# Local attention: which of two engines copies which head's transposed probabilities

## What is computed

```
h = layernorm(x)
lin_out = linear_attention(h @ wq_lin + bq_lin, h @ wk_lin + bk_lin, h @ wv_lin + bv_lin)
win_out = window_attention(h @ wq_loc + bq_loc, h @ wk_loc + bk_loc, h @ wv_loc + bv_loc, rel_bias)
gate = sigmoid(relu(concat(lin_out, win_out, h) @ wg1 + bg1) @ wg2 + bg2)
y = (gate * lin_out + (1 - gate) * win_out) @ wo + bo + h_input

window_attention, 16 heads of 8, window 64:
  scores[w] = sum_d(q * k shifted by w - 32) / sqrt(8) + rel_bias      (w = 0..64, -inf outside)
  attn = softmax over w
  out  = sum_w attn[w] * (v shifted by w - 32)
```

## Time and profile before

| | us |
|---|---|
| median of 3 runs | 2643.94 (2643.81 to 2646.72) |
| the profiled execution, device time | 2649.69 |
| its span, first to last instruction | 2646.9 |
| TensorE busy in it | 2476.4 (94%) |
| VectorE busy | 1937.0 (73%) |
| ScalarE busy | 1616.3 (61%) |
| GpSimd busy | 1147.0 (43%) |

### The profile page before, as it was taken

The page is one execution under the profiler, slowest core; times in us unless marked ns, Lnnn a source line. Parts: engine busy times, 40 slices in busy tenths (PEclk is TensorE's granted clock), DMA queues, the critical chain, the costliest instruction groups (busy, mean ns, idle before and its releaser), DMA issues. The chain is left out here.

```text
span 2646.9 us, 37817 instructions
## 1 busy us (share of the span) xinstructions
PE 2476.4 (94%) x11190; PEld 1413.2 (53%) x11190; DVE 1937.0 (73%) x3923; ACT 1616.3 (61%) x3503; POOL 1147.0 (43%) x924
## 2 busy tenths in 40 slices
PE   7999989899999999999989999988879998899977
PEld 5767754455555555555434444466644445556655
DVE  7888867799999999999956445466634444587754
ACT  4565533688888888888833344477734443466644
POOL 1000012499999999999930002022200001354532
PEclk8999989899999999999999999999989998999999
DMA  2000024344444444444443211000011110000000
GB/s 109 1 1 1 0 88 97 116 162 162 162 166 161 161 161 160 160 161 160 160 147 75 102 75 64 1 1 1 1 49 64 64 64 28 1 1 0 1 1 17
DMA packets 34771, 205.70 MB, mean 78 GB/s; under 512 B 4016, under 2 KB 5168, under 8 KB 13360
## 3 DMA queue, kind: packets, MB, share of 16 engines
q1 hardware_dynamic: 34608, 203.83, 21.7%
HBM read 201.19 MB, written 2.62 MB: 77 GB/s over the span
## 5 line engine op out<-in xcount | busy, mean ns | idle before, releaser
L1512 POOL TENSOR_TENSOR mam_state_c<-mam_state,weights_r 128x1024 f32<-128x1024 f32 x256 | 599.8, 2362 | 11.0 <-DVE mam_state L1474 9.8
L1474 DVE TENSOR_TENSOR_SCAN mam_state<-banks,mam_dbu 128x1024 f32<-128x1024 f32 x256 | 577.0, 2274 | 2.2 <-ACT banks L1543 1.3
L1593 PE MATMUL banks<-mam_state_c,identity 128*128 128x512 f32 x1024 | 483.2, 604 | 13.5 <-POOL mam_state_c L1512 12.9
L1543 ACT ACTIVATE banks<-mam_dt,mam_a_neg 128x255 f32<-128x255 f32 x1024 | 425.0, 461 | 64.3 <-DVE mam_state L1474 63.8
L1593 PEld LDWEIGHTS banks<-mam_state_c,identity 128*128 128x128 f32 x1024 | 186.5, 190 | 226.2 <-issue 189.6
L1021 PE MATMUL banks<-route_xnt,weights_r 128*128 128x512 f32 x512 | 245.0, 602 | 1.9 <-PEq L732 1.1
L1457 DVE TENSOR_TENSOR mam_dbu<-banks,weights_r 128x1024 f32<-128x1024 f32 x192 | 227.5, 1198 | 0.0
L432 ACT ACTIVATE at_probs<-banks,at_nmax 128x256 f32<-128x256 f32 x256 | 117.7, 472 | 139.4 <-DVE at_nmax L373 139.4
L552 POOL TENSOR_SCALAR route_ln_rs<-route_ln_mv 128x4 f32<-128x4 f32 x16 | 5.1, 317 | 453.0 <-DVE route_ln_mv L630 453.0
L2695 POOL TENSOR_TENSOR at_attention<-at_relu 128x512 f32<-128x512 f32 x128 | 131.0, 1040 | 127.3 <-ACT at_relu L2740 85.7
L969 DVE TENSOR_TENSOR m2b_hidden<-m2b_gelu,m2b_comb_spread 128x512 f32<-128x512 f32 x120 | 80.7, 690 | 116.4 <-ACT m2b_gelu L999 113.8
(11 more groups left out here) (433 smaller groups left out, 5027.8 us busy)
## 6 DMA issues: line engine op xcount, KB each, us to landing
weights_r<-mam_bc_rows SPq DMA_DIRECT2D x128, 1024.0 KB, 4.7
m2a_comb_spread<-m2a_comb_rows SPq DMA_DIRECT2D x15, 1024.0 KB, 6.9
m2b_comb_spread<-m2b_comb_rows SPq DMA_DIRECT2D x15, 1024.0 KB, 7.8
m1a_comb_spread<-m1a_comb_rows SPq DMA_DIRECT2D x14, 512.0 KB, 7.6
m1b_comb_spread<-m1b_comb_rows SPq DMA_DIRECT2D x14, 512.0 KB, 7.3
weights_r<-in_mb SPq DMA_DIRECT2D x1, 4332.0 KB, 13.0
weights_r<-in_m SPq DMA_DIRECT2D x1, 4200.0 KB, 12.8
weights_r<-in_a SPq DMA_DIRECT2D x1, 2632.0 KB, 11.9
```

Source lines behind the costliest of these rows:

```text
L1474: dve.tensor_tensor_scan(flat2(h[:, i % 4, :, :, :]), decay(i), flat2(dbu[:, i % 4, :, :, :]), 0.0, ALU.mult, ALU.add).then_inc(h_ready, 1)
L1512: pool.tensor_tensor(hc[:, j % 4, :, :, :], h[:, j % 4, :, :, :], c_rows(j), ALU.mult).then_inc(hc_ready, 1)
L1543: i = act.activation(decay(j)[:, o + 1:o + S], dt[:, q, c, 1:S], ACT.Exp, scale=aneg[:, l, k:k + 1])
L1593: k = pe.matmul(y_bank(q)[:, :], K.ident[:, :], flat(hc[:, j % 4, n, :, :]), start=(j == 0 and n == 0), stop=(j == NP - 1 and n == 1))
```

## The change

`BY_DVE`, the heads that VectorE copies, becomes the odd heads. Before they were 1, 4, 6, 9, 12 and 14 of each sequence; now they are 1, 3, 5, 7, 9, 11, 13 and 15. `BY_ACT` is what is left, so ScalarE copies the even heads, 0 to 14, in place of 0, 2, 3, 5, 7, 8, 10, 11, 13 and 15. As head h is transposed into bank 4 + h % 2, VectorE now reads bank 5 alone and ScalarE bank 4 alone. The slots, the copies' shapes and the banks stay. `wait_copied` and the two waits ahead of the product with the values go by these tuples and follow.

```diff
         TAIL = 15
-        BY_DVE = tuple(h for h in range(H) if h % 8 in (1, 4, 6))
+        BY_DVE = tuple(h for h in range(H) if h % 2)
         BY_ACT = tuple(h for h in range(H) if h not in BY_DVE)
```

## The result

The changed kernel takes 2668.45 us, the median of its four runs (2666.98 to 2669.76), against 2643.94 for the kernel before. A few executions of either kernel run in a slower state (one of before took 2927.95 us), and all medians and ratios here are of the others. A second comparison on another occasion gave 2665.79 us and 1.0084 (1.0071 to 1.0097), or 22.2 us. The forecast was 2661.5 in a range from 2649 to 2674. Sign and range held; of 22 to 25 us it had found 17.8. The profiled execution of the second comparison took 2660.96 us, the shortest of its six, so the traces show less of the loss than the medians do.

A forecast was written before the change was run, and what follows sets the result against it. The prediction took TensorE as pacer, in fixed order, standing still where VectorE or ScalarE comes late. Its terms, 10.0 + 0.4 + 7.4 = 17.8 us on the median 2643.94, gave 2661.5 us, range 2649 to 2674.

The forecast's parts named there:

- Slots 13 to 0, +1.0: Head 11's copy delays head 14's reduction; with head 12's copy on ScalarE, masked keys and next scores come 1.0 us later.
- Slots 0 to 4, +1.05: Head 15's copy delays the key-value sum; slot 4's scores come 2.0 us later, 1.0 of it already there at slot 0.
- The term of 5 x 2.0: Slot 13 to slot 4 costs 2.0 us in each of five sequence changes that are no loop boundary.
- Slots 5 to 7, +0.95: Copies of heads 3 and 4 delay ScalarE's output rows, the gate's first product and slot 8's scores: 0.95 us per sequence.
- 8 to 10, +0.1: Head 6's copy precedes the layer norm's output on ScalarE, but the gate's activation loses head 7's: 0.1 us per sequence.
- The boundaries, 2 x 0.2: Slots 13 to 4 at two loop boundaries: 0.2 us each, as TensorE's own delay covers most of VectorE's; bounds -1.3, +2.0.
- The eighth sequence and the tail, 0 with bounds of 0.6: First sequence and tail change copies only where a swap costs what it gives: nothing, bounds -0.6 to +0.6 us.
- The rival that saw the level fall in every sequence: TensorE's new pauses lower its clock in every sequence, 9.5 us more over five sequences: 2671 us, chance 0.2.
- only the two loop boundaries fall so far: Argument against the clock falling in every sequence: until now TensorE's level falls at the two loop boundaries alone.
- Absorption: Only the delay behind head 15 holds, 1.5 us in five sequences; ScalarE's reordered copies cost nothing: 2652 us, chance 0.15.
- relieved where it was late: ScalarE makes masked keys 0.48 us earlier and boundaries lose their wait on head 14: -9.8 us, 2634 us, chance 0.08.
- something moved: Answers the rival that nothing moves, swaps cancelling or only busy times balancing: 2644 us, chance 0.07.

The follow-up runs named there:

- second profile of after: The changed kernel, unchanged, run and traced once more: 2665.79 us, ratio 1.0084 to the kernel before.
- the experiment with head 15 alone: The kernel before, with only head 15's copy moved from ScalarE to VectorE: 2647.99 us, ratio 1.0014.
- head 15 back: The changed kernel with head 15's copy returned to ScalarE: 2660.28 us, ratio 1.0057 to the kernel before.
- heads 11 and 12 back: The changed kernel with head 11's copy returned to ScalarE and head 12's to VectorE: 2661.01 us, ratio 1.0054 to the kernel before.
- the keys moved with head 13 for 14: The kernel before with all masked keys in slot 14, the layer norm's output in slot 3, head 13 copied by VectorE and 14 by ScalarE: 2645.97 us.
- eight copies elsewhere: The kernel before with VectorE copying heads 1, 4, 5, 6, 7, 9, 12 and 13: 2644.71 us, ratio 1.0005.
- the second profile of before: The kernel before, unchanged, run and traced once more: 2643.56 us, ratio 0.9996.
- the kernel with head 13 for 14: The kernel before with head 13's copy moved to VectorE and head 14's to ScalarE: 2646.79 us, ratio 1.0006.

## Why the prediction was right, and where its sum fell short

**Slots 13 to 0, +1.0.** Right. Measured +1.37 and +0.79 in turn, 1.08 in the mean of six. In the +1.37 sequences head 14's exponential starts 0.88 us later in the stretch and not 0.52, because VectorE's update of x slips 0.36 us as well; with ScalarE's copy of head 12 (0.48) that gives the 1.37.

**Slots 0 to 4, +1.05.** Right: +1.02. The step from the key-value product to its copy was put at 2.25 us and measured 2.28; the wait before the scores of slot 4 at about 1.6 and measured 1.56.

**The sum where it can be checked.** From the second sequence's first scores to the eighth's, the prediction's terms make 14.7 us, and the traces show 15.2. This part was right by its mechanism and not by luck.

**The term of 5 x 2.0.** The five crossings that are no boundary measure 1.67, 2.40, 2.39, 2.41 and 1.23 us (each the surplus of slots 12 to 0 and of the next slots 0 to 4): 10.1 us against 10.0. The middle ones lie above, the first and the last below.

**Slots 5 to 7, +0.95, and 8 to 10, +0.1.** The first was right: +0.94, with each link within 0.1 us of its working (the exponential +0.60 for 0.52, the output rows +0.94 for 1.0). The second was small and had the wrong sign, -0.04. For the second to the seventh sequence the two make 5.3 us against the 6.3 of the sum.

**The boundaries, 2 x 0.2.** The first crossing cost 0.95 us and the second gained 0.09 (in the second profile of after 0.76 and 0.19): 0.9 in all against 0.4, where the two profiles of before differ by 0.25 themselves, well inside the bounds of -1.3 and +2.0. The reading was half right. VectorE did hold TensorE, but not by head 15's copy first: the first to wait was ScalarE, on the maximum of head 0, for a second pause of VectorE. The earlier trace rows show one pause at each boundary (5.6 us in two times); before has the second too, as its second profile shows at one boundary (1.47 us); at the others it would lie inside a wait for TensorE, which no row can show.

**The eighth sequence and the tail, 0 with bounds of 0.6.** This is the term that failed. The prediction put 1.0 us on slots 0 to 4 of this sequence, 1.05 on slots 4 to 12 and nothing on what follows, by the reasoning that there the change only swaps copies at equal cost; and it let VectorE's copy of head 13 cost nothing. The last sequence isn't like the others: VectorE has the next stage's normalisation in slot 5 and its routing weights behind the copy of head 13 in slot 15. Before and after differ here by 6.2 us in the first traces (56.55 against 50.32) and by 2.7 in the second (52.82 against 50.13), where the terms make 2.05. What repeats in both is idle time of TensorE in the last stretch, 12.0 us for 10.3 to 10.5, with the wait of 2.20 us for the routing weights in it; the rest moves with the clock. Restoring the old order there alone gave back 7.1 us of the median, more than before and after differ by, for the reason given at that kernel. So this term explains 0.6 to 4.2 of the 4 to 7 us that are missing from 17.8. What is left is not found in these traces, and the medians hold executions that no trace shows.

**The clock.** The rival that saw the level fall in every sequence was wrong where it was meant: the pauses came (1.29, 0.78 and 1.56 us in one sequence), and the granted clock stayed at 1.00 in each stretch. The section of the Trainium skill that the prediction named ("TensorE: Matmul & The Clock Gate", "HAM oscillation — how this bites in real kernels") tells of a kernel that pays the fall at the pause of every turn; this trace doesn't show that for its pauses of 0.8 to 1.6 us, and has, behind the first sequence, a lower clock only at the boundaries and from the eighth sequence on (0.84 at a boundary, 0.69 in the last stretch). The prediction's reading that in the kernel before "only the two loop boundaries fall so far" was incomplete: it falls in slots 8 to 12 of the eighth sequence too (0.86), behind a pause of 2.22 us. The same pause stands in the kernel with the last sequence copied as before, and there these slots stay at 1.00: the length of one pause doesn't decide it. In the last stretch the clock is worth 3.8 us between two executions of the same kernel. How much of the 7.1 us comes through it, once the order has let it fall, stays open.

**The other rivals.** Absorption was wrong for the crossings and right in kind for the boundaries, whose two sequences were no longer than before in the experiment with head 15 alone (64.09 us against 64.26 and 64.75). ScalarE was not relieved where it was late: its wait for the maximum of head 14 is the 1.26 us above. And something moved.

## What to carry to other kernels

Whether a copy can change its engine is read from what is queued behind it in its slot, not from mean shares: head 11's, 3's and 15's copies each stood before a reduction or a sum that the other engines waited for, and cost 1.0 to 1.5 us each per sequence, while eight copies in other slots made a sequence 1.0 us shorter than before. Read the sequences that aren't like the others (the last one, with the next stage's work in it, and those at a loop's jump) by their own rows; here 15 us of the loss were found slot by slot, and 3 to 6 us lay in the one sequence that was taken as like the rest, where a copy that is free everywhere else (head 13's) stands before the next stage's work. A gain in every sequence is worth little until the boundary sequences have been read too, with the stretch behind the boundary: in four of the kernels here (head 15 back, heads 11 and 12 back, the keys moved with head 13 for 14, eight copies elsewhere) they gave back two fifths to all of it or more.

## What was not expected of the hardware

- At the loop's jump VectorE stands still in two pieces, not one: 2.36 and 1.87 us in after, 2.72 and 1.47 in the second profile of before, 2.81 and 1.67 in the kernel with head 13 for 14, and in one piece of 4.69 in the kernel with eight copies elsewhere:

```profile
1793.64 0.32 DVE L1959 CUSTOM_DVE_ANT_0 at_scores<-banks,weights_r 128x160 f32<-128x160 f32 x1 [4.69 <-issue]
```

  That is 4.2 to 4.7 us in sum at the first boundary (4.0 at the second in after: 2.34 and 1.66). Where the pieces fall differs, and with it who waits. Their cause isn't shown by any row.
- The last stretch took from 24.8 us at a granted clock of 0.91 to 33.0 at 0.60, in before and in the kernel with head 13 for 14, and 27.1 or 30.9 in one and the same kernel. TensorE's busy time accounts for 6.1 of the 8.3 us between the first two (20.59 - 14.47); the rest, 2.15, is about the wait for the routing weights.
- Pauses of TensorE of 0.8 to 1.6 us, five in a sequence of 31 us, did not lower its clock (1.00 in each stretch).
